# Cross-attention with a feed-forward layer: the values matmuls of a phase in three runs instead of four

## The reference

```python
x = x + xattn(layernorm(x), ctx)        # this part holds the change
x = x + ffn(layernorm(x))               # eight experts, two per token, and a dense part

def xattn(ref_feat, sup_feat):
    sup = relu(sup_feat @ W_fc.T + b_fc)
    ref = relu(ref_feat @ W_fc.T + b_fc)
    q, k = heads(ref @ W_q.T + b_q), heads(sup @ W_k.T + b_k)
    p = softmax(q k^T / sqrt(16))
    return ref + concat over heads h of (p[h] @ sup) @ Wv[h].T + b_v
```

## Time and profile before

| | us |
|---|---|
| median of 3 runs | 1353.21 (1352.47 to 1355.25) |
| the profiled execution, its own time | 1355.13 |
| span of the profiled execution | 1353.4 |
| TensorE busy in it | 1261.2 |
| VectorE busy | 742.2 |
| ScalarE busy | 679.2 |
| GpSimd busy | 241.4 |

### The profile page before, as it was taken

One profiled execution on the slowest core, in us unless ns is written; L12 is line 12 of the kernel. 1 busy time (PEld: TensorE's weight loads), 2 busy tenths in 40 slices (PEclk: granted clock), 3 DMA queues, 4 the chain that ended last, 5 costly groups with the idle time before them and its releaser, 6 DMA issues. The chain is left out here.

```text
span 1353.4 us, 22244 instructions
## 1 busy us (share of the span) xinstructions
PE 1261.2 (93%) x8100; PEld 872.1 (64%) x8101; DVE 742.2 (55%) x1550; ACT 679.2 (50%) x938; POOL 241.4 (18%) x236
## 2 busy tenths in 40 slices
PE   4699999999999999999999999999588999999992
PEld 3567777777777777777777777555235556666661
DVE  4256676767677667766767767777144111112213
ACT  3337666666666666666666666555331112222220
POOL 3311112111111111211111111000025402222121
PEclk9889999999999999999999999999889999999996
DMA  4656454565445645456544563450299201111115
GB/s 137 211 162 150 128 144 113 135 158 152 112 133 132 145 131 148 114 126 159 147 122 133 127 141 114 96 120 14 71 242 395 79 16 46 44 46 44 47 43 198
DMA packets 154910, 168.36 MB, mean 124 GB/s; under 512 B 69040, under 2 KB 140344, under 8 KB 154816
## 3 DMA queue, kind: packets, MB, share of 16 engines
q1 hardware_dynamic: 151360, 157.61, 44.5%
q0 software_dynamic: 3456, 9.47, 1.9%
HBM read 103.55 MB, written 63.31 MB: 123 GB/s over the span
## 5 line engine op out<-in xcount | busy, mean ns | idle before, releaser
L602 DVE TENSOR_REDUCE mx<-side 128x1 f32<-128x400 f32 (+1 forms) x1024 | 534.5, 570 | 139.9 <-PE side L454 130.8
L497 ACT ACTIVATE prob<-st 128x1024 f32<-128x1024 f32 (+1 forms) x416 | 411.8, 1023 | 183.2 <-PE st L475 182.1
L454 PE MATMUL side<-kst,qst 96*128 96x400 f32 (+1 forms) x1024 | 329.1, 382 | 3.7 <-DVE mx L602 2.4
L475 PE MATMUL st<-qst,kst 97*128 97x512 f32 (+1 forms) x832 | 265.0, 401 | 5.9 <-ACT prob L497 3.5
L454 PEld LDWEIGHTS side<-kst,qst 96*128 96x128 f32 x1024 | 189.6, 189 | 113.9 <-issue 37.5
L487 PE MATMUL acc<-prob,v 128*32 128x256 f32 (+1 forms) x3328 | 207.6, 385 | 0.0
L475 PEld LDWEIGHTS st<-qst,kst 97*128 97x128 f32 (+1 forms) x832 | 148.3, 186 | 18.2 <-ACT prob L497 8.9
L487 PEld LDWEIGHTS acc<-prob,v 128*32 128x32 f32 (+1 forms) x3328 | 95.7, 110 | 79.6 <-issue 24.4
L634 POOL TENSOR_TENSOR clo<-raw,chi 128x768 fp32r<-128x768 f32 (+1 forms) x32 | 60.8, 1901 | 450.0 <-ACT chi L528 450.0
L1429 DVE TENSOR_TENSOR hg<-sg,pu 128x512 f32<-128x512 f32 x40 | 27.5, 688 | 139.7 <-PE pu L1607 139.7
L640 POOL TENSOR_TENSOR flo<-fc,fhi 128x768 fp32r<-128x768 f32 (+1 forms) x32 | 61.1, 1910 | 214.8 <-ACT fhi L541 214.8
(11 more groups left out here) (162 smaller groups left out, 1407.1 us busy)
## 6 DMA issues: line engine op xcount, KB each, us to landing
kst<-parts_at SPq DMA_DIRECT2D x90, 400.2 KB, 5.8
parts_at<-parts SPq DMA_DIRECT2D x48, 384.0 KB, 5.9
v<-v_at SPq DMA_DIRECT2D x32, 408.0 KB
raw<-ctx_t SPq DMA_DIRECT2D x24, 384.0 KB, 3.3
v_at<-vst SPq DMA_DIRECT2D x32, 272.0 KB
wall<-gate_up SPq DMA_DIRECT2D x8, 1024.0 KB, 14.1
parts_at<-parts SPq DMA_DIRECT2D x16, 449.0 KB, 2.7
qst<-q_at SPq DMA_DIRECT2D x192, 32.0 KB, 5.9
```

The source lines that it names most:

```text
L454: pe.matmul(side[u.bank][:, 0:w], t.qst[0:96, pair, col * P:(col + 1) * P], t.kst[0:96, pair, o:o + w], start=True, stop=True).then_inc(si ...
L475: mm = pe.matmul(into[0:rows, i * 2 * NQ:(i + 1) * 2 * NQ], t.kst[0:97, GP * g + i, s * P:s * P + rows], t.qst[0:97, GP * g + i, :], start ...
L497: act.activation(prob[0:rows, s, :], st[(KT * g + s) % 2][0:rows, :], ACT.Exp, scale=float(DH) ** -0.5).then_inc(exp_done, 1)
L602: dve.tensor_reduce(mx[:, hq, r:r + 1], side[u.bank][:, 0:RANGES[r][1]], AX.X, ALU.max)\
```

## The change

The items of `STEP` are moved. Behind it a phase has the runs: tiles 0 to 4 at step 8, between its two score tiles; 5 to 8 at step 12; 9 to 12 at step 4 of the next phase. No values matmuls stand at steps 7 and 10. The matmuls, their operands and their number are the same. The loop after the last phase begins at tile 9.

```diff
--- before.py
+++ after.py
@@ -66,15 +66,15 @@
     ["S", "v 0", "S", "0 xturn 1"],
     ["S"],
     ["S", "S", "v 1", "S", "chi", "S"],
-    ["S", "S", "prev 8", "prev 9", "prev 10", "prev 11", "prev 12", "accout", "S", "0 xchi"],
+    ["S", "S", "prev 9", "prev 10", "prev 11", "prev 12", "accout", "S", "0 xchi"],
     ["S", "S", "f 0", "S", "S"],
     ["S", "f 1", "S", "S"],
-    ["fhi", "S", "out", "V 0", "V 1", "S"],
-    ["S", "S", "0 xfc"],
+    ["fhi", "S", "out", "S"],
+    ["S", "V 0", "V 1", "V 2", "V 3", "V 4", "S", "0 xfc"],
     ["S", "S"],
-    ["1 xp", "S", "1 xres", "V 2", "V 3", "V 4", "V 5", "tm", "S"],
+    ["1 xp", "S", "1 xres", "tm", "S"],
     ["S", "S"],
-    ["S", "S", "V 6", "V 7", "S", "S", "S"],
+    ["S", "S", "V 5", "V 6", "V 7", "V 8", "S", "S", "S"],
 ]
 ORDER = [x for step in STEP for x in step]
 AHEAD = ORDER[ORDER.index("tm"):].count("S")
@@ -1018,7 +1018,7 @@
                                     pe_out(pe, body_unit(b, at, g, kind, arg), p - 1)
 
                 batches(pe, body)
-                for kt in range(8, KT):
+                for kt in range(9, KT):
                     pe_values(pe, PHASES - 1, B - 1, GROUPS - 1, kt)
                 pe_out(pe, Unit(AT_END), PHASES - 1)
```

## The result

The changed kernel takes 1401.22 us (median of 4 runs, 1400.94 to 1402.69) against 1353.33 for the kernel before: a ratio of 1.0354, 95% interval 1.0339 to 1.037. The change costs 48 us; 34 were forecast, and the range ended at 1400. The profiled executions have spans of 1399.3 and 1353.4 us. The 45.9 us between them are 2 less than between the medians, since the profiled execution of the kernel before was 1.8 us above its own median.

What follows compares the result with a forecast made beforehand. TensorE's instruction stream was taken as the path. 24 ordinary turns cost 25.9 us, less 3.0 won back, plus 10.8 for seven long turns: 33.7 us on the median of 1353.21, so 1387 us; range 1378 to 1400.

Steps and rivals of the forecast that it cites:

- the turn waits: Step 10: the matmul `tm` waits for VectorE's row maxima, about 1.1 us in ordinary phases, over 2 us in seven.
- The distances of 1.45 and 2.95 us: From the last score tile to the turn: 1.42 us in ordinary phases, 2.95 us in the seven with query projection.
- The 0.19 us of steps 9 and 10: Time won back on TensorE as ScalarE's three exponentials are broken up; 16 ordinary phases and the seven.
- the successor's 0.07 us: Step 10: behind a wait the turn holds up its next instruction 0.10 us instead of 0.03, 0.07 more.
- rival 3: Idleness at the seven long turns lowers the clock: 2 to 7 us each, 14 to 49 us, 1401 to 1436; chance 6%.
- steps 7 and 8: A score tile follows `out`, a run of five comes one score tile later: nothing, at most 0.05 us a phase.
- the entry and exit of the two runs: The run removed at step 7 and the one added at step 8 both have an entry and exit; these cancel.
- Rival 1: The turn waits for nothing and one run less in 31 phases saves 4 to 10 us: 1343 to 1349; chance 4%.
- Rivals 2 and 4: 2: both effects cancel, 1351 to 1356 us, chance 3%. 4: same mechanism, smaller, 1370 to 1378 us, chance 10%.
- the row's way back: ScalarE's copy of the maxima and DMA to the query stack: cover grows 0.87 us; copy delay at most 0.1 us.

Runs made afterwards that it cites:

- g1_cover: The changed kernel with values tiles 1 to 4 back ahead of the turn of the maxima in the eight phases of group 1; 1.0209 times the kernel before.
- g1_bare: The kernel before with the run of tiles 2 to 5 moved from ahead of the turn to step 8, in group 1's eight phases only; 1.0193 times before.
- g1_two: The changed kernel with values tiles 3 and 4 put between the residual and the turn in group 1's eight phases; 1.0251 times the kernel before.
- split_run: The changed kernel with step 12's run of tiles 5 to 8 split by one score tile into two runs of two; 1.040 times the kernel before.
- twice_after: The changed kernel with VectorE's reduce of the four partial maxima done twice; 1.0377 times the kernel before.
- turn_step12: The changed kernel with the turn of the maxima moved from step 10 to the head of step 12; 1.0347 times the kernel before.
- four_five_four: The changed kernel with its three runs placed otherwise: tiles 0 to 3 at step 7, 4 to 8 ahead of the turn, 9 to 12 at step 4; 1.0105 times before.
- three_moved: four_five_four with three of step 12's five score tiles moved to steps 0 and 2 of the next phase; 1.0271 times the kernel before.

## Why the prediction was wrong, point by point

**What bounds the kernel** held: TensorE's stream was the path and took every wait in full.

**The direction and the mechanism** held: the turn waits in all 31 phases, 1.11 or 1.02 us in the ordinary ones (about 1.1 forecast) and 1.97 in seven (over 2), 39.5 us in all (some 40). The distances of 1.45 and 2.95 us were forecast as 1.42 and 2.95. The 0.19 us of steps 9 and 10 came back, and the successor's 0.07 us were paid.

**A row was misread**, without harm: the earlier trace rows has 596 us for TensorE's weight loads, and VectorE's busy time is 588 us, 71% of the stretch.

**The step that failed is rival 3, the clock,** which the sum and the range's upper end put at nothing. Its price was put at 14 to 49 us, 2 to 7 at each turn, and its chance at 6%; it came at six turns, at 1.7 or 3.4 us each, 11.8 us in all. Without it the time would have been about 1390, inside the range. The evidence on which the chance rested was read badly. The idleness of 1.41 us in the feed-forward part with the clock up answers for the ordinary turns, 1.1 us, and is right for them; it says nothing on 2 us. TensorE has two waits of that size in the trace of before, from 90 us on, and they disagree. One is that of the earlier trace rows, in a stretch at a mean clock of 0.79. It spoke for the rival but does not prove it, since half clock had begun there ahead of the wait, in a row of score tiles that follow each other at VectorE's pace, 0.48 us (84.15 to 93.28 us, 19 tiles), with no idleness above 0.2 us:

```profile
84.15 8.94 PE L454 MATMUL side<-kst,qst 96*128 96x400 f32 x19
```

```profile
90.00:95.00 5.00, 4.81 (x11) 2.83 (x10) 4.87 (x11) 0.00 (x0) 0.00 (x0) 0.50 0.00 0
```

The other was left out of account. It is in the dense feed-forward part, and the clock stays up behind it:

```profile
1017.83 7.17 PE L1568 MATMUL py<-wb,h 128*128 128x256 f32 x32 [2.17 <-POOL h L1198]
```

```profile
1015.00:1025.00 10.00, 7.83 (x38) 6.76 (x37) 8.52 (x30) 2.24 (x5) 3.48 (x4) 1.00 1.05 411
```

So the trace of before neither showed nor excluded a fall after 2 us of idleness, and a chance near one half for these seven turns, or an upper end of the range above 1401, would have been the honest reading. g1_cover, g1_bare and g1_two show that the falls belong to the seven waits, and that each of these brings it about often but not always.

**The sum without the clock** was 33.7 us; 49.3 less 11.8 is 37.5 between the turns (38.9 with the 10.4 us that the distances give), so 3.8 to 5.2 us are missing in the sum. They lie in steps 7 and 8, which I cost at nothing, at most 0.05 us. From behind `out` to step 9's scores it took 2.12 us with two tiles (514.05 to 516.17), 1.25 us beside them; now it takes 3.61 with five (537.04 to 540.65 above), 1.44 beside 5 x 0.433. That is 0.19 us in this phase, 0.20 in the next and 0.10 in the one after, which has `0 xfc`. Over 24 phases at 0.19 and seven at 0.10 it is 5.3 us, as much as the distances leave open. I had let the entry and exit of the two runs cancel. They don't: the run at step 7 stood directly behind the transposes of `out`. The new run stands between two score tiles, and a score tile stands behind the transposes. By the starts, the three score tiles of this stretch take 0.84 us (0.29 behind the transposes, 0.27 ahead of the run, 0.28 behind it) instead of 0.64. That each such change on TensorE has its price, and that a run directly behind the transposes shares theirs, is read from these rows and was not tried by itself.

**Rival 1**, the saving of a run a phase, is real and small: 0.14 us by split_run. The page "TensorEngine Tiling (Array Packing)" of the Trainium skill says in Key Properties that a change of mode drains the array; the extra time at the ends of a run agrees, but by that rule alone the change would have been a gain.

**Rivals 2 and 4** did not come. No new wait stands at steps 4 and 12 or on the row's way back, so the claim that the other edits are free was not contradicted. Behind the last turn the changed kernel has 1.9 us less. There the kernel before has a mean clock of 0.91 from 945 to 975 us, the changed one 1.00 from 990 to 1020; but the profiles differ in this part by more than that.

## What to carry to other kernels

When a block of work on the bounding engine is moved, ask first what it covers where it stands: the end of the other engines' answer against the moment at which the in-order queue needs it. Then count by stretches between such blocks, each engine's work against the others', since moving the waiting instruction inside a stretch only moves the wait. If the new waits are as long as one around which the trace shows the lower clock, put the lower clock into the range, even if another wait of that length left it alone.

## What the runs showed of the hardware that I had not expected

TensorE's clock fell to 1.2 GHz behind waits of 1.97 us, six times in seven in two kernels that differ in all other phases, with TensorE otherwise busy nearly without a break, and stayed at 2.4 GHz behind waits of 1.11 and 0.98 us. In split_run (1.98 us) and twice_after (2.07 us) it fell at five of the seven, and in turn_step12 at five turns with 1.3 us of idleness and several shorter waits behind it. In twice_after it also fell once behind an ordinary turn, in the one phase in which that turn's idleness was 1.5 us and not 1.2.

A wait of 2 us does not decide it. The feed-forward part's wait of 2.17 us, shown above for the kernel before, stands in the profiles of all 13 kernels behind the same instructions. In nine the clock stays up behind it; in four (g1_two, four_five_four, twice_after, three_moved) it falls, behind the wait or at its end. The same instruction and the clock in g1_two:

```profile
1046.35 8.86 PE L1568 MATMUL py<-wb,h 128*128 128x256 f32 x32 [2.17 <-POOL h L1198]
```

```profile
1045.00:1055.00 10.00, 8.65 (x32) 7.34 (x33) 9.05 (x30) 1.15 (x3) 3.47 (x4) 0.83 1.05 406
```

So with the same wait and the same work around it the clock can fall or stay. Why some of the long turns were spared, the first of the seven each time, was not tried and stays open.

A run of 32-column matmuls directly behind fp32 transposes came 0.19 us a phase cheaper than one between two score matmuls with the transposes ahead of a score tile. What is shared there was not tried.
